# Gates sent to the experts' rows through memory, and four smaller edits, in a three-stage decoder layer

## The reference, cut to what matters

```python
# 1: causal self attention, 16 heads of 16
qkv = x @ w_qkv + b_qkv
att = softmax(where(causal, q @ k.T / sqrt(16), -inf));  y = (att @ v) @ w_proj + b_proj
# 2: three iterations over the same context, "slots" = the text
Pn = rmsnorm(ctx, input_norm_w); k_proj = Pn @ Wk.T; v_proj = Pn @ Wv.T
for _ in range(3):
    scores = (rmsnorm(slots, slot_norm_w) @ Wq.T) @ k_proj.T * SCALE
    attn = softmax(scores, axis=-2); attn = attn / (sum(attn, -1) + EPS)
    slots = gru_cell(attn @ v_proj, slots, ...)
# 3: 16 experts of 64, the best 4 by sigmoid count
sel_val, sel_index = top_k(sigmoid(x @ expert_sel.T), 4); sel_val /= sum(sel_val)
scores_all = relu(einsum('btd,edh->bteh', x, keys))
out = sum over the 4 selected of sel_val * (scores_all @ values)
```

## Time and profile before

| | |
|---|---|
| median of 3 runs | 675.24 us (673.99 to 680.57) |
| profiled execution | 674.05 us, its span 672.3 us |
| TensorE busy in the span | 630.6 us (94%) |
| VectorE, ScalarE, GpSimd busy | 497.9, 340.5, 223.4 us |
| mean granted TensorE clock | 0.991 of 2.4 GHz |

### The profile page before, as it was taken

How to read it: one execution, slowest core, us unless ns; L and a number is a source line. 1 busy time by engine, 2 the same in 40 slices (tenths; PEclk the granted TensorE clock), 3 DMA queues, 4 the chain that set the end, 5 groups by cost and what they waited for, 6 DMA issues and landing times.

```text
span 672.3 us, 14159 instructions
## 1 busy us (share of the span) xinstructions
PE 630.6 (94%) x5144; PEld 577.2 (86%) x5160; DVE 497.9 (74%) x1045; ACT 340.5 (51%) x758; POOL 223.4 (33%) x272
## 2 busy tenths in 40 slices
PE   5889998997989999999999999999999987999996
PEld 5766776776768999999999999999999986999996
DVE  4754666565754888879888798897989978676663
ACT  4434545453674455754556645556466544153350
POOL 9303335233453323213222223123231116062542
PEclk9899999899999999999999999999999998999999
DMA  8635556258300220000000000000000000000000
GB/s 282 204 96 169 148 162 203 77 181 215 78 19 1 75 83 1 16 17 2 0 0 16 16 0 0 0 0 0 0 1 2 0 2 0 17 18 32 0 32 32
DMA packets 24271, 36.96 MB, mean 55 GB/s; under 512 B 2208, under 2 KB 11808, under 8 KB 24224
## 3 DMA queue, kind: packets, MB, share of 16 engines
q1 hardware_dynamic: 24224, 36.34, 18.1%
HBM read 23.10 MB, written 13.11 MB: 54 GB/s over the span
## 4 chain that ended last, share of the span: by engine, by line
PE 56%; issue 13%; DVE 13%; POOL 5%; SPq 5%; DMA 5%; ACT 2%; another core or an unknown queue 1%; DVEq 0%; POOLq 0%; ACTq 0%
PE bank L433 26%; PE bank L2127 11%; PE bank L1946 5%; POOL hid_hl L762 4%; DMA k_rows<-k_hl 3%; PE bank L1955 2%; DMA q_op<-negT 2%; PE bank L441 2%; PE bank L1964 1%; PE bank L1932 1%; PE bank L1846 1%; SPq L503 1%; DVE neg_max L1254 1%; PE bank L1812 1%; PE bank L1827 1%
## 5 line engine op out<-in xcount | busy, mean ns | idle before, releaser
L433 PE MATMUL bank<-slots_hl,whhT_hl 128*128 128x256 f32 x864 | 113.8, 284 | 0.0
L433 PEld LDWEIGHTS bank<-slots_hl,whhT_hl 128*128 128x128 f32 x864 | 106.2, 188 | 2.5 <-ACT gate_z L1065 1.0
L2127 PE MATMUL bank<-attn_hl,vg_hl 128*128 128x256 f32 x864 | 107.0, 282 | 0.0
L1254 DVE TENSOR_REDUCE neg_max<-bank 128x2 f32<-128x512 f32 (+1 forms) x96 | 65.5, 690 | 53.4 <-PE bank L1814 37.4
L2127 PEld LDWEIGHTS bank<-attn_hl,vg_hl 128*128 128x128 f32 x864 | 102.6, 189 | 0.2 <-POOL attn_hl L672 0.2
L831 ACT ACTIVATE pT<-bank 128x512 f32<-128x512 f32 x96 | 56.9, 598 | 53.2 <-PE bank L1827 37.7
L643 POOL TENSOR_SCALAR_AFFINE_SELECT pT<-pT 128x512 f32<-128x512 f32 x64 | 40.5, 636 | 116.3 <-ACT pT L831 116.2
L657 POOL TENSOR_TENSOR sq<-sq 128x256 f32<-128x256 f32 x24 | 18.1, 753 | 172.8 <-ACT sq L1050 130.8
L762 POOL TENSOR_TENSOR hid_hl<-hid,hid_hl 128x512 fp32r<-128x512 f32 x32 | 41.1, 1303 | 32.7 <-ACT hid_hl L776 32.4
L433 PE MATMUL bank<-x2T_hl,keys_hl 128*128 128x256 f32 x384 | 50.3, 285 | 0.3 <-ACT hid L1139 0.3
L433 PE MATMUL bank<-values_hl,hid_hl 128*128 128x256 f32 x384 | 49.1, 286 | 0.3 <-DVE x L1530 0.3
(11 more groups left out here) (209 smaller groups left out, 1332.9 us busy)
## 6 DMA issues: line engine op xcount, KB each, us to landing
q_rows<-q_hl SPq DMA_DIRECT2D x21, 256.0 KB
k_rows<-k_hl SPq DMA_DIRECT2D x21, 256.0 KB
q_op<-q_rows SPq DMA_DIRECT2D x28, 192.0 KB, 3.2
k_op<-k_rows SPq DMA_DIRECT2D x14, 384.0 KB, 4.8
x_in<-in_x_dram SPq DMA_DIRECT2D x8, 256.0 KB, 6.5
c_in<-in_ctx_dram SPq DMA_DIRECT2D x8, 256.0 KB, 4.7
out_dram<-y_out SPq DMA_DIRECT2D x8, 256.0 KB, 2.1
xT_in<-in_xT_dram SPq DMA_DIRECT2D x3, 512.0 KB, 5.7
```

Source lines behind the costliest of these rows:

```text
L433: mm = pe.matmul(dst, left(a), right(b), start=first and n == 0, stop=last and n == 2, skip_group_check=True)
L1254: dve.tensor_reduce(dst, src, AX.X, ALU.max, negate=True).then_inc(max_ok, 1)
L2127: mm = pe.matmul(halves(b)[:, m, :], vg_hl[:, j, v_part, 3 * t + r, q:q + P], attn_hl[:, j, at_part, t, :], start=n == 2 and a + m + t == ...
```

## The change

Five things change.

1. **Gates through memory** in rounds 1 to 3 of the experts. The eight `gb` jobs of a round (16 products) are gone. ScalarE copies the turned gates of a batch to `gateT` (`gates_whole`), SyncE writes them to `gate_mem` in DRAM (16 KB), waits for that, and issues eight transfers that read them back with each expert's row repeated over 64 partitions, into `gate_rows` (1 MB for a batch, 1 KB for each contiguous piece). VectorE takes relu and gate in one instruction (`scalar_tensor_tensor`, max with 0, then times `gate_rows`) straight from the bank of the hidden units. ScalarE's `relu` and VectorE's `gates_lo` are gone in these rounds. The hidden units have four banks instead of two (4 + n % 4).
2. **Order** around it: `gT` of both batches and `route` of the second come earlier.
3. **Scales** in the cross stage: `pe.transpose` in place of `pe.matmul` with the same operands.
4. **Full rows**: `q_op` and `k_op` have 128 partitions instead of 97, the added rows zero (`q_op`) or one (`k_op`); the turned products (and only these) run over all 128. GpSimd clears `q_op`'s added rows at the start (two more memsets).
5. **Heads**: VectorE divides both halves of a batch's heads in one go, where a maximum stood between.

```diff
-        q_op = sb("q_op", [K_ROWS + 1, 2, 2, H // 2, T], F32R, where=sq_op)
+        q_op = sb("q_op", [P, 2, 2, H // 2, T], F32R, where=sq_op)
...
+            def gates_by_memory(i, j):
+
+                sp.wait_ge(gT_hi, due(2, i, j + 1))
+                sp.sem_inc(passed, 1)
+                sp.dma_start(gate_mem[j, :, :], gateT[:, j, :]).then_inc(gates_out[j], 16)
+                sp.wait_ge(gates_out[j], due(1, i, 0, step=16))
+                sp.sem_inc(passed, 1)
+                for g in range(4):
+                    for e in range(2):
+                        sp.dma_start(gate_rows[EH * e:EH * (e + 1), j, 2 * g:2 * g + 2, :],
+                                     gate_mem[j, :, :].rearrange("(m e) t -> e m t", e=2)[e, 2 * g:2 * g + 2, :].partition_broadcast(EH)
+                                     ).then_inc(gates_in[j][g // 2], 16)
...
+            with sp.Fori(0, PAIRS - 1) as i:
+                gates_by_memory(i + 1, 0)
+                store(i, 0)
+                gates_by_memory(i + 1, 1)
+                store(i, 1)
...
+            for e in range(2):
+                pool.memset(f32(q_op[K_ROWS:, 0, e, :, :]), 0.0).then_inc(rows_ok, 1)
+            pool.wait_ge(rows_ok, 2)
...
+            def gates_whole(i, j, b):
                 act.wait_ge(gT_mm, due(2, i, j + 1))
+                act.wait_ge(gates_out[j], due(1, i, 0, back=1, step=16))
+                copy(gateT[:, j, :], bank[b][0:NE, 0:T]).then_inc(gT_hi, 1)
...
                         inverse_sums(2 * period - 1)
                         heads(2 * period - 1, 0)
-                    elif key == (2, 0) and 0 <= 2 * period - 1 < B:
                         heads(2 * period - 1, 1)
...
+                    dve.scalar_tensor_tensor(hid[:, n % HIDDEN, :, :], halves(4 + n % 4), 0.0, gate_rows[:, j, 2 * g:2 * g + 2, :],
+                                             ALU.max, ALU.mult).then_inc(h_ok, 1)
...
                     if j and not last:
-                        gates_lo(i + 1, 0, 0)
+                        route(i, i + 1, 1)
...
-                    mm = pe.matmul(bank[b][:, t * P:(t + 1) * P], s_rs[:, j, t:t + 1].to_broadcast([P, P]), ident[:, :],
-                                   start=True, stop=True)
+                    mm = pe.transpose(bank[b][:, t * P:(t + 1) * P], s_rs[:, j, t:t + 1].to_broadcast([P, P]), ident[:, :])
```

More of the change, by code:

```diff
@@ L145, in decoder_layer @@
         rs_bc = sb("rs_bc", [P, 2, T])
+        sg = ExitStack()
+        gate_rows = sb("gate_rows", [P, 2, NH, T], where=sg)
+        sg.close()
         attn = sb("attn", [P, 2, NT, T])
@@ L501, in maxima @@
                 sp.wait_ge(neg_ok, hh + 1)
+                after(sp, rows_ok, 2 if hh == 0 else 0)
                 for e in range(2):
@@ L1146, in hidden_hi @@
                     copy(hid_hl[:, j, HI, 2 * g:2 * g + 2, :], hid[:, n % HIDDEN, :, :]).then_inc(h_hi, 1)
-                hidden_hi(0)
-                if not first:
-                    gates_hi(i, 1, 1)
-                hidden_hi(1)
-                relu(i, 4)
-                if not first:
-                    hidden_hi(2)
-                relu(i, 5)
-                if first:
-                    gates_hi(0, 1, FIRST_TEXT[1])
-                    hidden_hi(2)
-                hidden_hi(3)
-                relu(i, 6)
-                if not (last or first):
-                    expert_text_hi(i + 1, 0, 0)
-                hidden_hi(4)
-                relu(i, 7)
-                if first:
-                    expert_text_hi(i + 1, 0, 0)
+                if first:
+                    hidden_hi(0)
+                    hidden_hi(1)
+                    relu(i, 4)
+                    relu(i, 5)
+                    gates_hi(1)
+                    hidden_hi(2)
+                    hidden_hi(3)
+                    relu(i, 6)
+                    hidden_hi(4)
+                    relu(i, 7)
+                    expert_text_hi(i + 1, 0, 0)
+                else:
+                    for n in range(4):
+                        hidden_hi(n)
+                    if not last:
+                        expert_text_hi(i + 1, 0, 0)
+                    hidden_hi(4)
                 hidden_hi(5)
@@ L1171, in experts @@
                     exp_logits(i + 1, 0, 0)
-                    gates_hi(i + 1, 0, 0)
+                    gates_whole(i + 1, 0, 0)
                     exp_logits(i + 1, 1, 1)
-                    for n in range(4):
-                        relu(i + 1, n)
+                    gates_whole(i + 1, 1, 1)
             relu(0, 0)
@@ L1180, in _ @@
             exp_logits(0, 1, FIRST_TEXT[1])
-            gates_hi(0, 0, FIRST_TEXT[0])
+            gates_hi(0)
             relu(0, 3)
@@ L1736, in experts @@
                     text(1, 1)
+                if not (first or last):
+                    expert_text_lo(i + 1, 0, 0)
                 gated(4)
@@ L1739, in experts @@
                     last_moments(1)
-                elif not last:
-                    expert_text_lo(i + 1, 0, 0)
                 gated(5)
@@ L1762, in experts @@
                     moments(i, expert_chain, EXPERT_LINKS, lambda t: u3[:, t, :], stats3, mv3, std3, var3)
-                    if j and not last:
-                        route(i, i + 1, 1)
                     normal(i, lambda t: u3[:, t, :], mv3, std3, rstd3, j + 1, lambda t: y_out[:, j, t, :], y_ok)
@@ L1824, in turned @@
                     pe.wait_ge(neg_in[hh % 2], 32 * (hh // 2 + 1))
+                    after(pe, rows_ok, 2 if hh == 0 else 0)
                 after(pe, exp_ok, fill - 1)
@@ L2199, in experts @@
                         continue
-                    if first and (name, n) == ("gT", 1):
+                    if name == "second gT":
                         pe.wait_ge(lx_ok, due(2, 0, 2))
@@ L2206, in experts @@
                         pe.wait_ge(x2_ok, due(2, PAIRS - 1, 1 if name == "tT" else 2))
-                    b, read, count = bank_free(jobs3, i, (name, n), last)
+                    b, read, count = FIRST_FREE[name, n] if first and name in ("h", "gb") else bank_free(jobs3, i, (name, n), last)
                     if name != "o":
```

62 lines of the change are left out of this document (39 added, 23 removed), and 3 rows, old and new, of the table EXPERT_ORDER.

## The result

The kernel after took 666.95 us (median of 4 runs, 663.9 to 669.5) beside 675.5 us for the kernel before: ratio 0.987, 95% interval 0.9832 to 0.9908. Six more runs of it, beside eleven of before, gave 664.7 against 675.6 us: 0.9838 (0.9805 to 0.9871). So the change is worth 8.5 to 11 us, about 10. The forecast was 661.5, within 656 to 668.5.

A forecast was written before the change was run, and what follows sets the result against it. TensorE was taken to bound the experts and cross stage, with holes only in attention. Experts 7.0, scales 5.2, rows 0 and heads 1.3 make 13.5 us off the profiled 674.05; median 1.2 above: forecast 661.5 us, range 656 to 668.5.

The forecast's parts named there:

- the first rival: Experts: gate rows come a little late, so they gain 1 to 2 us instead of 7: 666.5 to 667.5; chance 0.10.
- the low clock: Attention stage: its clock of 0.98 may make some 1.5 us come or go, allowed for in the range.
- Experts, -7.0 us: Gates through memory: two middle rounds 2.0 us shorter each, the last 3.0; bounds 4.5 to 8.5 us.
- Nothing waits: Middle expert round: second batch's rows in by H + 11.8, `gated(4)` at about H + 12; H is the first `h`'s start.
- Scales, -5.2 us: Cross stage: transposes take two passes instead of four, 0.22 us less, 24 times; bounds 3.5 and 5.5 us.
- so also a unit that is paced by a wait gets shorter by it: Cross stage: each dependence loop runs from one `scales` to the next, so every unit gains the 0.22 us.
- a third is lost: Cross stage: lower bound of 3.5 us for the scales, a third of the gain ending in other waits.
- Full rows, 0: Attention stage: 128 rows instead of 97 change nothing, the 0.08 us belonging to the step; bounds -0.5 to +1.
- The rival's 128 places: Attention stage: full rows save 0.08 us at each of 128 products, all of it felt: 651 us; chance 0.06.
- Heads, -1.3 us (0 to 2.5): Attention stage: four TensorE waits for the second division, 2.5 us, go; two are swallowed by waits for memory.
- The clock: Cross stage: transposes don't count as activity, so a tenth runs at 1.2 GHz, losing 13.6 us: 675 us; chance 0.03.
- The slower rival: Experts: from 1.4 us an issue SyncE becomes the bound, 16 us lost over three rounds: 677 us; chance 0.04.

The follow-up runs named there:

- experiments 1 and 2: Scales as float32 matmuls again on the kernel after: 666.7 us; transposes for the scales alone on the kernel before: 673.8 us.
- `a_16loads`: Kernel after with each of the eight loads of gate rows of a batch cut in two: 696.2 us, ratio to before 1.029.
- `b_heads`: Kernel before with the second division of the heads moved up alone: mean 673.6 us against 675.8 for before.
- `a_rows97`: Kernel after with the 97-row operands of before, no added rows or memsets: mean 668.2 us against 665.8 for after.

## Why the prediction was right or wrong

The direction and the range held; the forecast was about 4 us too fast against all ten runs, because one term of the sum was three times too large. The range held with some luck. The median of 666.95 lies outside the forecast's own bounds (656.5 to 666) and inside the part that was added for the first rival and the low clock. It even falls on that rival's 666.5 to 667.5, but not by its mechanism, for the experts kept nearly all of their gain. (The lower bounds of the four parts add up to 7.5 us, not 8, and both bounds were taken from the profiled execution, 1.2 us below the median.)

- **Experts, -7.0 us: nearly right as a sum, by two errors that cancel.** The two traces of after have 7.1 and 6.8 us; over ten traces the mean is 83.4 us against 89.9 for three with the experts of before, 6.6 us. Two middle rounds were to give 2.0 us each. Without their holes they take 26.6 us in the median, close to the forecast's 26.5, but with them 27.1 in the mean, so each gives 1.4. The last round was to give 3.0 us and gave 3.6 to 3.9: it took 22.75 to 23.2 us from its first `h` to TensorE's last product, where I had 23.6. The step that failed in the middle rounds is "Nothing waits". I had the second batch's rows in at H + 11.8; they are in at H + 13.9, because its write stands behind the first batch's eight loads and a store on SyncE (612.38, H + 4.0, loads from H + 6.3 instead of H + 4.6) and a load takes 3.1 us to land where I took 2.1. What was listed as queued behind the loads, "only the stores", left out the second batch's own write. VectorE waits for them in most rounds, and TensorE loses 0.5 us a middle round at `gT`; how much of that is the rows' and how much the rest of `route`'s chain was not separated.
- **Scales, -5.2 us: wrong, 1.3 to 1.7 us.** The price of two passes was right: where the inputs wait for nothing, as in the second unit of the second round, it was 0.36 us from the scales to the inputs (314.31 before) and is 0.13 (316.12 after). The second trace of after and the experiments 1 and 2 give the same 1.3 to 1.7 us for the stage. The failed step is "so also a unit that is paced by a wait gets shorter by it". It holds for a loop that runs through the scales. The chain from mean squares by `s_ms`, weights and copy to the inputs runs beside them, under the cover of scores and scales, and sixteen of the 23 distances gained nothing. The bound of 3.5 us ("a third is lost") had the mechanism, and too small a share. That the cover had no slack could have been read from the trace of before: inputs at 255.57 and the end of ScalarE's copy at 254.86 + 0.63 = 255.49.
- **Full rows, 0: right**, by the step (315 ns with either); the timed runs allow 0 to 2 us. The rival's 128 places were too many: in the trace of after, 84 of the 128 turned products follow a mask product.
- **Heads, -1.3 us (0 to 2.5): the mechanism right, the size too small**, 2.3 to 2.8 us in the timed runs, that is all of the 2.5 us of waits. I had taken half of them for swallowed by the waits for memory; no trace shows these to grow with the edit.
- **The clock.** The cross stage stayed at 1.00 with the transposes, two in a unit of 11 to 18 us. The Trainium skill says that transposes don't count as activity ("TensorE: Matmul & The Clock Gate", Part 4); these few did not put that rule to the test, and no run here has more of them. The allowance of 1.5 us for the low clock in the attention stage was too narrow: its traces have from 6.8 to 23.9 us of it, at 0.48 us each.
- **The slower rival: real, and nearer than I put it.** "It decides at about 1.3 us an issue", with 16 us lost over three rounds at 1.45. In `a_16loads` the eight pieces of a batch took 10.09 us, 1.26 us each; by my count that is 8 x (1.26 - 0.64) - 1 = 4 us a round and 12 in all, and 30 were lost. I had costed lateness against the slack of one wait. But a middle round got 10 us longer, as much as its issues: the queue, VectorE's gates, the low parts and the next round's routing are one loop, and the low clock came on top in the pauses. How the 30 us divide between the loop and the clock was not separated.

The sum with the measured terms, 6.6 + 1.5 + 0 + 2.5 = 10.6 us, stands beside a measured difference of the means of 675.8 - 665.8 = 10.0 +- 0.7 us. The 8.5 us of the first comparison are within its interval. What stays open: why the time of the transfers through memory and of the low clock in the attention stage vary so from run to run. In the runs the mean clock was 0.989 for before, 0.987 for `b_heads` and 0.982 for `a_rows97`; that a fuller attention stage brings more of the low clock was not tested.

## What to carry to other kernels

When work is taken off the bounding engine, ask for each place what else ends there within that time: a product that is also the cover of a chain on other engines gives back only the slack of that chain, and one look at the releaser of the next instruction tells it. In an in-order queue, an early wait for one thing (`s_ms`) delays what stands behind it (the weights), and turning the two round may only move the wait; starting the follower in halves shortened the chain, and most of that was kept. Many small transfers through one queue are to be counted by issues, not bytes, with everything that queues behind them; where they are only just in time, as here, all of an added 10 us of issues a round went into the round. And when a term of a sum comes out right, look at its parts: here two of them were wrong in opposite directions.

## What the runs showed of the hardware

A transfer's issue on SyncE took 0.60 us for 64 KB and for 128 KB alike (both in rows of 1 KB, spread over 64 partitions). A write of 16 KB to memory and the next load of it, which waits for the write, were issued 1.5 to 3.4 us apart, and a load of 128 KB landed 3.1 us behind its issue. A float32 product by a transpose instruction left one record where a matmul left two (48 and 96 for the scales), and the difference, 0.22 us for two instructions of 128 columns, was felt only where the next product waited for nothing. A copy of 128x512 to float32r on ScalarE took 0.63 us, two of 128x256 took 0.81 together.
